# Attention and mixture-of-experts block on one core: the last batch's attention shares its slots with the first 38 dense units

## The chip, the cores and the metric

One core of a Trainium2 chip. The metric is the device time of one launch in microseconds (us). The engines are TensorE (PE; its weight loads are shown as PEld), VectorE (DVE), ScalarE (ACT), GpSimd (POOL) and SyncE (SP), which here only issues DMAs. Each engine takes its instructions strictly in program order; a semaphore wait holds everything behind it on its engine.

## What is computed

Four batches of 256 tokens with 256 channels (`x`, and a side input `f` of the same shape). Shortened:

```
# bi-directional WKV: two linear scans over the tokens, forward and backward
ek = exp(min(f, 30)); ekv = ek * f
nf, df = forward scans of ekv, ek;  nb, db = backward scans
num = nf + nb - ekv + exp(min(u + f, 30)) * f;  den = df + db - ek + exp(min(u + f, 30))
wkv(x) = sigmoid(x) * num / max(den, 1e-8) * (0.8 + 0.2 * tf)

qkv = wkv1(x) @ Wqkv.T + bqkv                     # 16 heads of 16 channels
x = x + softmax(q k.T * 4) v @ Wproj.T + bproj
h = wkv2(x)                                       # same scans with other w, u
scores = sigmoid(h @ gate_w.T)                    # 64 experts, 8 groups
w = best 6 experts out of the 4 best groups, normalised, times 2.5
x = x + sum_e w_e * relu(h @ w1_e.T)**2 @ w2_e.T + relu(h @ up.T)**2 @ down.T
```

All experts are computed for all tokens, each weighted by `w` (zero where it is not chosen).

## The kernel before

**Layout and stages.** Channels lie on the partitions, in two chunks (KC = 2), tokens in the free dimension. Batch b's scans feed two "hidden" tensors: `hid1` (attention input) and `hid2` (dense input). Each engine has its own hand-written instruction list; the order in these lists is the schedule.

**Attention.** `project` (L1129) makes q, k and v of a batch, 8 matmul instructions each. ACT rounds q and k to `qk_hi` (`evacuate_qk`, L495); DVE takes the low parts `qk_lo` (`split_qk`, L772) and adds the bias of v (`add_v_bias`, L785). SP stacks high and low parts in `q_st`/`k_st` (three slots of 8 heads). Per head there is `scores` (L1140, two matmuls), `maximum` on DVE (L796), `shifted_scores` (L1159, the scores again with the negative maximum added by two extra rows), `probabilities` on ACT (L511), and once per four heads `values` (L1172, 16 instructions). `scores` of head n waits for `maximum` of head n-2, since two PSUM banks take turns. After a batch: `turn_out`, `normalise`, `turn_normalised`, `evacuate_o_ch`, `project_out`, `residual`, `second_exp`, `second_rec`, `hidden2`, `gate`, `gate_exp`, `router` (32 DVE steps for one batch, 256 tokens), `turn_weights`, `evacuate_w`. This is called the tail of a batch here. Batch b's tail, and the second half of its heads, run while batch b+1's first half is made; the second scans of batch b+1 and the first scans of b+2 are spread between the maxima.

**Dense part.** 34 tiles of 128 intermediate channels (2 shared, 32 with two experts each), each applied to two halves of 512 tokens: 68 units. Unit n: SP loads the raw weights and the spread gates (`load_unit`); ACT rounds the weights (`split_hi`, L567) and DVE takes the rest (`split_lo`, L949); PE `up` (L1258 to L1260, 6 matmuls of 512 columns); ACT `rectify` (L574); POOL `square` (L446); DVE `gated` (L1053, times gates); ACT `round_act` (L581); DVE `low_act` (L1058); PE `down` (L1269 to L1271, 6 matmuls), two units later. The order of one unit's turn is, on every engine:

```
PE   up(n), down(n-2)
ACT  rectify(n), round_act(n-1), split_hi(n+2)
POOL square(n)
DVE  low_act(n-1), gated(n), split_lo(n+2)
```

The dense part begins when all attention scores of batch 3 are done; the first 18 units (HEAD) also hold the tail of batch 3, with three router steps behind each unit. Then loops of four units run to the end. `result` adds the sums to x1, and SP stores the output.

Of the kernel before, what the change touches and what calls it, by code (L numbers as in the profile page):

```python
# [17 lines left out]
P = 128  # L18
B, S, C = 4, 256, 256
# [12 lines left out]
HEAD = 18  # L32
# [7 lines left out]
RING = 4  # L40
PRING = 8
# [15 lines left out]
def bass_adaln_attn_ffn(nc, xT, fT, cond, vecs, w_in, w_out, gate_w, bv, gate_bias, tiles, out):  # L57
# [3 lines left out]
    with ExitStack() as ctx:  # L61
# [12 lines left out]
        cond_sb = sb("cond_sb", [P, B, TD])  # L74
# [22 lines left out]
        ekv = sb("ekv", [P, KC, S])  # L97
# [10 lines left out]
        ones = sb("ones", [2 * SHARED * B, S])  # L108
        zeros = sb("zeros", [MAXROW - STACK, S])
# [9 lines left out]
        o_ch = sb("o_ch", [P, KC, S])  # L119
# [3 lines left out]
        hid2 = sb("hid2", [P, KC, S])  # L123
        hid_hi = sb("hid_hi", [P, KC, TOK], F32R)
        hid_lo = sb("hid_lo", [P, KC, TOK], F32R)
        gex = sb("gex", [P, QT, E])
        gden = sb("gden", [P, QT, E])
        score = sb("score", [P, QT, E])
        sbias = sb("sbias", [P, QT, G, EG])
        pmax = sb("pmax", [P, QT * G, 4])  # L130
        pmin = sb("pmin", [P, QT * G, 4])
        qmax = sb("qmax", [P, QT * G, 2])
        qmid = sb("qmid", [P, QT * G, 2])
        qlow = sb("qlow", [P, QT * G, 2])
        qsec = sb("qsec", [P, QT * G, 2])
        fmax = sb("fmax", [P, QT * G, 1])
        fmid = sb("fmid", [P, QT * G, 1])
        flow = sb("flow", [P, QT * G, 1])
        fsec = sb("fsec", [P, QT * G, 1])
        gsum = sb("gsum", [P, QT, G + 4])  # L140
        gtop = sb("gtop", [P, QT, 8])
        grep = sb("grep", [P, QT, G + 4])
        gpen = sb("gpen", [P, QT, G])
        masked = sb("masked", [P, QT, E + 2])
        etop = sb("etop", [P, QT, 8])
        erep = sb("erep", [P, QT, E + 2])
        wsel = sb("wsel", [P, QT, E])
        wsum = sb("wsum", [P, QT])
        wsum1 = sb("wsum1", [P, QT])
        wrec = sb("wrec", [P, QT])  # L150
        wful = sb("wful", [P, QT, E])
        w_ch = sb("w_ch", [E, TOK])
# [3 lines left out]
        t_hi = k_st[:, 2].rearrange("p (k n) s -> p k (n s)", k=RING)  # L156
        t_lo = q_st[:, 2].rearrange("p (k n) s -> p k (n s)", k=RING)
# [8 lines left out]
        ones_ready, ld_ones = sem("ones_ready"), sem("ld_ones")  # L166
# [37 lines left out]
        def bank_s(n):  # L204
            return ps[:, n % 2, :].rearrange("p (t k) -> p t k", t=QT)
# [43 lines left out]
        def bank_h(k):  # L249
            return ps[:, k, :]  # L250
# [1151 lines left out]
```

## Time and profile before

| | us |
|---|---|
| median of 3 runs | 408.05 (405.69 to 408.51) |
| the profiled execution | 405.65 |
| its span, first to last instruction | 403.8 |
| PE / DVE busy in it | 317.7 (79%) / 322.9 (80%) |
| ACT / POOL busy | 201.2 (50%) / 129.5 (32%) |
| mean granted clock of TensorE | 0.897 of full speed |

The profile gives busy time by engine, the busy share in 40 slices of the span, the chain of work that ended last, and the costliest groups of instructions. Durations of neighbouring instructions on one engine overlap by some 0.07 us, so the distance from start to start is the cost of one, and that is what is used below. The granted clock is 1.0 where TensorE ran at 2.4 GHz and 0.5 where it ran at 1.2 GHz.

### The profile page before, as it was taken

Reading aid. Unit: us, or ns where it says so; the run is one execution under the profiler, and the core shown is the slowest. Engines: PE = TensorE matmul, PEld = TensorE weight load, DVE = VectorE, ACT = ScalarE, POOL = GpSimd, SP = SyncE. Lnnn points to the kernel's source line nnn. Section 1 sums busy time; section 2 is a strip of 40 time slices with the busy share of each in tenths; the row PEclk is TensorE's granted clock in tenths of the full one; section 3 lists DMA queues with packets and bytes.
Section 4 is the critical chain, followed back from the end, with each engine's and each line's share of the span. In section 5 each row is a group of like instructions: output and inputs, shape, how many; then the busy total and the mean of one; then the engine's idle time right before and its main releaser. Section 6 shows DMA issues by size and latency. Waiting matters only on the chain.

```text
span 403.8 us, 6023 instructions
## 1 busy us (share of the span) xinstructions
PE 317.7 (79%) x1552; PEld 244.3 (61%) x1552; DVE 322.9 (80%) x623; ACT 201.2 (50%) x373; POOL 129.5 (32%) x117
## 2 busy tenths in 40 slices
PE   0071369677954897768988897999999999999994
PEld 0050247455733585545666675888888788888882
DVE  6979997986699477886568995888888888888883
ACT  4112125434552256466455553666666666656651
POOL 3428443306061002011322342434334334334331
PEclk9995559758985798997999998999999999999999
DMA  6959707803380068300543444566556666656531
GB/s 199 164 71 119 166 2 93 111 11 52 55 106 2 13 94 105 108 10 24 173 144 117 157 168 145 163 188 192 194 181 194 177 200 188 199 182 191 195 139 52
DMA packets 36150, 50.89 MB, mean 126 GB/s; under 512 B 5218, under 2 KB 17954, under 8 KB 36130
## 3 DMA queue, kind: packets, MB, share of 16 engines
q1 hardware_dynamic: 36130, 50.65, 51.4%
q8 instruction: 9, 0.15, 0.2%
q14 instruction: 11, 0.09, 0.1%
HBM read 39.16 MB, written 1.33 MB: 100 GB/s over the span
## 4 chain that ended last, share of the span: by engine, by line
PE 54%; DVE 29%; issue 7%; ACT 5%; POOL 2%; DMA 1%; DVEq 0%; ACTq 0%; SPq 0%; POOLq 0%
DVE scan L731 7%; PE ps L1258 7%; PE ps L1260 7%; PE ps L1269 6%; PE ps L1271 6%; PE ps L1259 6%; PE ps L1270 6%; DVE mx L796 5%; PE ps L1129 4%; PE ps L1172 3%; PE ps L1140 2%; DVE q_st L949 2%; DVE scan L1053 2%; PE ps L1159 2%; DVE den L744 2%
## 5 line engine op out<-in xcount | busy, mean ns | idle before, releaser
L446 POOL TENSOR_TENSOR scan<-scan 128x512 f32<-128x512 f32 x68 | 73.2, 1076 | 137.9 <-ACT scan L574 136.2
L1058 DVE TENSOR_TENSOR qk_lo<-scan,qk_hi 128x512 fp32r<-128x512 f32 x68 | 69.3, 1019 | 31.3 <-ACT qk_hi L581 31.3
L574 ACT ACTIVATE scan<-ps 128x512 f32<-128x512 f32 x68 | 40.7, 598 | 49.8 <-PE ps L1260 49.6
L1140 PE MATMUL ps<-k_st,q_st 96*128 96x256 f32 x128 | 35.6, 395 | 30.8 <-DVE mx L796 20.3
L1269 PE MATMUL ps<-qk_hi,k_st 128*128 128x512 f32 x136 | 54.7, 402 | 4.5 <-DVE qk_lo L1058 4.3
L1258 PE MATMUL ps<-hid_hi,k_st 128*128 128x512 f32 x136 | 54.4, 400 | 2.0 <-DVE q_st L949 2.0
L567 ACT ACTIVATE k_st<-clip 128x512 fp32r<-128x512 f32 x68 | 42.8, 631 | 25.3 <-PE ps L1271 25.3
L1260 PE MATMUL ps<-hid_hi,q_st 128*128 128x512 f32 x136 | 54.0, 397 | 0.0
L1271 PE MATMUL ps<-qk_hi,q_st 128*128 128x512 f32 x136 | 53.7, 395 | 0.0
L1270 PE MATMUL ps<-qk_lo,k_st 128*128 128x512 f32 x136 | 53.6, 394 | 0.0
L1259 PE MATMUL ps<-hid_lo,k_st 128*128 128x512 f32 x136 | 53.6, 394 | 0.0
L511 ACT ACTIVATE prob<-ps 128x512 f32<-128x512 f32 x64 | 36.6, 593 | 33.5 <-PE ps L1159 33.0
L949 DVE TENSOR_TENSOR q_st<-clip,k_st 128x512 fp32r<-128x512 f32 x68 | 48.6, 716 | 2.6 <-ACT k_st L567 2.6
L1140 PEld LDWEIGHTS ps<-k_st,q_st 96*128 96x128 f32 x128 | 25.0, 255 | 40.9 <-DVE mx L796 27.9
L796 DVE TENSOR_REDUCE mx<-ps 128x2 f32<-128x512 f32 x64 | 42.6, 679 | 5.6 <-PE ps L1140 4.3
L1053 DVE TENSOR_TENSOR scan<-scan,ex 128x512 f32<-128x512 f32 x68 | 46.1, 679 | 0.2 <-DVE o_tok L816 0.2
L581 ACT ACTIVATE qk_hi<-scan 128x512 fp32r<-128x512 f32 x68 | 42.5, 624 | 2.8 <-DVE scan L1053 2.6
L1159 PE MATMUL ps<-q_st,k_st 98*128 98x256 f32 x128 | 33.5, 359 | 5.5 <-ACT prob L511 3.2
L1129 PE MATMUL ps<-hid,wi 128*128 128x256 f32 x64 | 20.3, 478 | 19.8 <-DVE hid L764 19.8
L1269 PEld LDWEIGHTS ps<-qk_hi,k_st 128*128 128x128 f32 x136 | 25.7, 189 | 14.5 <-DVE qk_lo L1058 8.2
L1258 PEld LDWEIGHTS ps<-hid_hi,k_st 128*128 128x128 f32 x136 | 25.8, 190 | 9.2 <-DVE q_st L949 3.5
L1159 PEld LDWEIGHTS ps<-q_st,k_st 98*128 98x128 f32 x128 | 24.6, 233 | 11.0 <-ACT prob L511 6.2
(117 smaller groups left out, 451.4 us busy)
## 6 DMA issues: line engine op xcount, KB each, us to landing
clip<-in_tiles SPq DMA_DIRECT2D x68, 256.0 KB, 3.1
ex<-gates SPq DMA_DIRECT2D x136, 128.0 KB, 2.9
q_st<-qk_hi SPq DMA_DIRECT2D x16, 128.0 KB, 3.9
q_st<-qk_lo SPq DMA_DIRECT2D x16, 128.0 KB, 4.5
k_st<-qk_hi SPq DMA_DIRECT2D x16, 128.0 KB, 5.3
k_st<-qk_lo SPq DMA_DIRECT2D x16, 128.0 KB, 6.2
f_sb<-in_fT SPq DMA_DIRECT2D x4, 256.0 KB, 8.8
x_sb<-in_xT SPq DMA_DIRECT2D x4, 256.0 KB, 9.6
```

The costliest lines, as they stand in the source:

```text
L446: g.tensor_tensor(sq[:, k], relu[:, k], relu[:, k], ALU.mult).then_inc(sq_ready, 1)
L796: v.tensor_reduce(mx[:, b % 2, h], bank_s(n), AX_X, ALU.max).then_inc(max_ready, 1)
L949: TT(t_lo[:, k], raw[:, k], t_hi[:, k].bitcast(F32), ALU.subtract).then_inc(t_lo_ready, 1)
L1058: TT(act_lo[:, k], act[:, k], act_hi[:, k].bitcast(F32), ALU.subtract).then_inc(act_lo_ready, 1)
L1140: last = mm(bank_s(n)[:, qt], q_st[0:MAXROW, slot(b, h // HB), h % HB, qt * P:(qt + 1) * P], k_st[0:MAXROW, slot(b, h // HB), h % HB, :], ...
L1159: last = mm(bank_t(n)[:, kt], k_st[0:MAXROW + 2, slot(b, h // HB), h % HB, kt * P:(kt + 1) * P], q_st[0:MAXROW + 2, slot(b, h // HB), h % ...
L1258: mm(bank_h(k), w_hi, x_hi, start=(c == 0), stop=False)
L1259: mm(bank_h(k), w_hi, x_lo, start=False, stop=False)
L1260: last = mm(bank_h(k), w_lo, x_hi, start=False, stop=(c == KC - 1))
L1269: mm(acc, w_hi, act_hi[:, k], start=first, stop=False, skip_group_check=True)
L1270: mm(acc, w_hi, act_lo[:, k], start=False, stop=False, skip_group_check=True)
L1271: last = mm(acc, w_lo, act_hi[:, k], start=False, stop=final, skip_group_check=True)
```

## The change

- The dense part's first 38 units no longer wait for batch 3's attention. Batches 0 to 2 run in 48 "slots", one head's `scores` and `maximum` in each. The 43 slots after that hold batch 3's 16 heads (slots 0 to 15) and units 0 to 37: unit n stands in slot n+4 (n < 2) or n+5. `shifted_scores`, `probabilities` and `values` lag `scores` by 10 slots.
- In those slots `scores` has a single PSUM bank (bank 0), so head n waits for the maximum of head n-1; `shifted_scores` has a single bank (2) from head 40 on; units 0 to 11 have a single bank (1) for `up`.
- The low parts of q and k of batches 1 to 3: PE subtracts the rounded part in PSUM (`subtract_high`: two matmuls with a negative identity), ACT evacuates (`evacuate_rest`). v's bias is added by a matmul, v evacuated by ACT.
- One router of the same steps for two batches (four token tiles): the first, `router(0)`, in slots 0 to 3 (6 steps each), the second in slots 33 to 36.
- The gates of a unit are loaded with one DMA, not two. Buffers are shared otherwise; the dense weights `t_hi`/`t_lo` have buffers of their own. `exponentials` is split and takes `clip[:, 3]` second; `ekv` lies in `clip[:, 3]`.
- The loops of four now cover units 38 to 65.

```diff
-HEAD = 18
+RT = 2 * QT
+LAG = 10
+ENTRY = 4
+GAP = 1
+ALONE = 12
+HEAD = NT + RING
...
         def bank_s(n):
-            return ps[:, n % 2, :].rearrange("p (t k) -> p t k", t=QT)
+            return ps[:, n % 2 if n < H * (B - 1) else 0, :].rearrange("p (t k) -> p t k", t=QT)
 
         def bank_t(n):
-            return ps[:, 2 + n % 2, :].rearrange("p (t q) -> p t q", t=QT)
+            return ps[:, 2 + n % 2 if n < H * (B - 1) - HB else 2, :].rearrange("p (t q) -> p t q", t=QT)
...
+        def unit_bank(n):
+            return n % 2 if n >= ALONE else 1
+
+        def unit_at(s):
+            n = s - ENTRY if s < ENTRY + SHARED else s - ENTRY - GAP
+            return n if n >= 0 and (s < ENTRY + SHARED or n >= SHARED) else None
+
+        def head_slot(n):
+            early = H + HB <= n < 2 * H
+            return H + HB + LAG + (n - H - HB) // 2 if early else n + LAG
+
+        def tail_slot(b):
+            return head_slot(H * b + H - 1) + 2
...
# SyncE
+            for n in range(RING, 2 * RING):
+                next_raw(n, n, n % RING)
             store_gates(0)
-            store_gates(1)
-            sp.wait_ge(st_gates, 32)
-            for n in range(RING):
+            for n in range(SHARED, RING):
                 load_spread(0, n, n)
...
# ScalarE
+            def evacuate_rest(b, w):
+
+                job = ("qk"[w], b)
+                sc.wait_ge(rest_ready, 2 * (b - 1) + w + 1)
+                for t in range(KC):
+                    u = (V_BQ, V_BK)[w] + t
+                    a.activation(qk_lo[:, w, t], job_bank(job)[:, t * S:(t + 1) * S], ACT.Identity,
+                                 bias=vec[:, u:u + 1]).then_inc(qk_lo_ready, 1)
...
+            for s in range(HEAD + ENTRY + GAP):
+                n = unit_at(s)
+                for m in shifted_at(H * (B - 1) + s):
+                    probabilities(m // H, m % H, m % H + 1)
+                if s < 2:
+                    split_hi(s, s, 1)
...
+                if n is not None:
+                    rectify(n, n % 2)
+                    if n > 0:
+                        round_act(n - 1, (n - 1) % 2)
+                    split_hi(n + 2, (n + 2) % RING, (n + 2) // RING + 1)
...
# VectorE
+            for g in range(H * (B - 1)):
+                b, s = g // H, g % H
+                maximum(b, s)
+                if s == 0:
+                    if b > 0:
+                        low_max(b - 1, 1)
+                    num_den(b + 1, 0, 0)
+                if s == 1:
+                    hidden1(b + 1)
+                if s == 2:
+                    scans(b + 1, 1, 1, 0)
...
+            route_now = router(0)
+            for s in range(HEAD + ENTRY + GAP):
+                n = unit_at(s)
+                if s < H:
+                    maximum(3, s)
+                if s == 0:
+                    low_max(2, 1)
+                if s < 2:
+                    split_lo(s, s)
+                if s < 4:
+                    for _ in range(6):
+                        next(route_now, None)
...
+                if n is not None:
+                    if n > 0:
+                        low_act(n - 1, (n - 1) % 2)
+                    gated(n, n % 2, n % RING, n // RING + 1)
+                    split_lo(n + 2, (n + 2) % RING)
...
# TensorE
+            def subtract_high(b, w):
+
+                job = ("qk"[w], b)
+                pe.wait_ge(qk_hi_ready, 4 * b + 2 * w + 2)
+                for t in range(KC):
+                    last = mm(job_bank(job)[:, t * S:(t + 1) * S], minus[:], qk_hi[:, w, t], start=False, stop=True,
+                              skip_group_check=True)
+                last.then_inc(rest_ready, 1)
...
-                    pe.wait_ge(max_ready, n - 1)
+                    pe.wait_ge(max_ready, n if n > H * (B - 1) else n - 1)
...
+            for g in range(H * (B - 1)):
+                b, s = g // H, g % H
+                for n in shifted_at(g):
+                    shifted_scores(n // H, n % H)
+                if g + 2 <= H * (B - 1):
+                    scores((g + 2) // H, (g + 2) % H)
+                for m in values_at(g):
+                    values(m // 4, m % 4)
+                if s == 2:
+                    project(b + 1, "q")
+                if s == 3:
+                    subtract_high(b + 1, 0)
+                if s == 4:
+                    project(b + 1, "k")
+                if s == 5:
+                    subtract_high(b + 1, 1)
...
+            for s in range(HEAD + ENTRY + GAP):
+                n = unit_at(s)
+                for m in shifted_at(H * (B - 1) + s):
+                    shifted_scores(m // H, m % H)
+                if s + 1 < H:
+                    scores(B - 1, s + 1)
+                if s == 4:
+                    turn_weights(0)
+                for m in values_at(H * (B - 1) + s):
+                    values(m // 4, m % 4)
...
+                up(n, n // NT, n % 2, n % RING)
+                if n >= 2:
+                    down(n - 2, (n - 2) // NT, n % 2, (n - 2) % RING, first=(n - 2) % NT == 0, final=n - 2 == NT - 1)
```

## Rows read from the trace of the kernel before

**Rows 1.** The page: PE's busy tenths in 40 equal slices, and granted TensorE clock

```profile
PE   0071369677954897768988897999999999999994
PEclk9995559758985798997999998999999999999999
```

**Rows 2.** Windows: busy us of PE, PEld, DVE, ACT, POOL; granted clock; DMA share

```profile
175.00:180.00 5.00, 3.08 (x28) 1.76 (x26) 3.93 (x13) 4.22 (x9) 0.33 (x1) 1.00 0.03 7
180.00:185.00 5.00, 3.52 (x20) 2.88 (x24) 2.42 (x6) 3.34 (x8) 2.20 (x2) 0.58 0.05 13
```

**Rows 3.** Timeline: first maxima of batches 0, 1, 3; first `up` matmul of units 0, 38, 67

```profile
42.48 0.68 DVE L796 TENSOR_REDUCE mx<-ps 128x2 f32<-128x512 f32 x1
...
74.77 0.68 DVE L796 TENSOR_REDUCE mx<-ps 128x2 f32<-128x512 f32 x1
...
155.27 0.68 DVE L796 TENSOR_REDUCE mx<-ps 128x2 f32<-128x512 f32 x1
...
192.89 0.50 PE L1258 MATMUL ps<-hid_hi,k_st 128*128 128x512 f32 x1
...
311.87 0.40 PE L1258 MATMUL ps<-hid_hi,k_st 128*128 128x512 f32 x1
...
392.19 0.40 PE L1258 MATMUL ps<-hid_hi,k_st 128*128 128x512 f32 x1
```

**Rows 4.** Timeline, DVE: two scans, a maximum, a stall at `split_qk`, a later maximum

```profile
43.08 1.26 DVE L731 TENSOR_TENSOR_SCAN scan<-ps,ex 128x256 f32<-128x256 f32 x2
44.26 0.66 DVE L796 TENSOR_REDUCE mx<-ps 128x2 f32<-128x512 f32 x1
...
62.70 0.88 DVE L772 SCALAR_TENSOR_TENSOR qk_lo<-ps,vec,qk_hi 128x256 fp32r<-128x256 f32 x2 [2.27 <-ACT qk_hi L495]
...
162.19 0.68 DVE L796 TENSOR_REDUCE mx<-ps 128x2 f32<-128x512 f32 x1
```

**Rows 5.** Timeline, PE: a `project`, `scores`, `shifted_scores`, `values`, the start of a tail

```profile
62.26 1.89 PE L1129 MATMUL ps<-hid,wi 128*128 128x256 f32 x8
...
162.93 0.50 PE L1140 MATMUL ps<-k_st,q_st 96*128 96x256 f32 x2 [0.17 <-DVE mx L796]
163.27 0.40 PE L1159 MATMUL ps<-q_st,k_st 98*128 98x256 f32 x2
...
165.58 1.07 PE L1172 MATMUL ps<-prob,v_aug 128*32 128x256 f32 x16
...
168.95 1.09 PE L1182 MATMUL ps<-ident,o_raw 128*128 128x128 f32 x8 [0.50 <-ACT o_raw L518]
```

**Rows 6.** Timeline, DVE: first and last step of a router of one batch

```profile
184.88 0.23 DVE L859 TENSOR_SCALAR gden<-gex 128x128 f32<-128x128 f32 x1 [2.49 <-ACT gex L549]
...
191.87 0.42 DVE L938 TENSOR_SCALAR wful<-wsel,wrec 128x64 f32<-128x64 f32 x2
```

**Rows 7.** Timeline of a dense unit in the steady part, all engines

```profile
300.79 0.40 PE L1258 MATMUL ps<-hid_hi,k_st 128*128 128x512 f32 x1
302.46 0.60 ACT L574 ACTIVATE scan<-ps 128x512 f32<-128x512 f32 x1 [0.78 <-PE ps L1260]
302.95 0.62 ACT L581 ACTIVATE qk_hi<-scan 128x512 fp32r<-128x512 f32 x1
303.13 1.04 POOL L446 TENSOR_TENSOR scan<-scan 128x512 f32<-128x512 f32 x1 [1.81 <-ACT scan L574]
303.61 1.11 DVE L1058 TENSOR_TENSOR qk_lo<-scan,qk_hi 128x512 fp32r<-128x512 f32 x1 [0.53 <-ACT qk_hi L581]
304.65 0.68 DVE L1053 TENSOR_TENSOR scan<-scan,ex 128x512 f32<-128x512 f32 x1
305.25 0.68 DVE L949 TENSOR_TENSOR q_st<-clip,k_st 128x512 fp32r<-128x512 f32 x1
```

**Rows 8.** Timeline, PE: two neighbouring matmuls of a unit at the low clock

```profile
246.24 0.63 PE L1269 MATMUL ps<-qk_hi,k_st 128*128 128x512 f32 x1
246.67 0.63 PE L1270 MATMUL ps<-qk_lo,k_st 128*128 128x512 f32 x1
```

More of the change, by code:

```diff
@@ new lines, in _ @@
+            for s in range(HB - 1, HEAD + 1):
+                if s + 1 >= 2 * RING and s + 1 < HEAD:
+                    n = s + 1
+                    next_raw(n, n % NT, n % RING)
+                n = s - 1
+                if n == NT + SHARED:
+                    store_gates(1)
+                if n >= RING + SHARED:
+                    next_spread(n, n // NT, n % NT, n % RING)
+                if s == HB - 1:
+                    load_rows(B - 1, 0)
+                if s == H - 1:
+                    load_rows(B - 1, 1)
@@ L571, in rectify @@
                 sc.wait_ge(h_ready, n + 1)
+                if isinstance(n, int) and n == 0:
+                    sc.wait_ge(numden_ready, 4 * B)
                 if not isinstance(n, int) or n >= 2:
                     sc.wait_ge(sq_ready, n - 1)
-                a.activation(relu[:, k], bank_h(k), ACT.Relu).then_inc(relu_ready, 1)
+                bank = unit_bank(n) if isinstance(n, int) else k
+                a.activation(relu[:, k], bank_h(bank), ACT.Relu).then_inc(relu_ready, 1)
             def round_act(n, k):
                 sc.wait_ge(act_ready, n + 1)
+                if isinstance(n, int) and n == 0:
+                    for half in range(KC):
+                        sc.wait_ge(ld_stack[slot(B - 1, half)], 128 * turn(B - 1, half))
                 if not isinstance(n, int) or n >= 2:
@@ L629, in _ @@
[L629 to L658 removed]
+                if s == 5:
+                    evacuate_rest(b + 1, 1)
@@ L1099, in loop @@
                         split_lo(n + 2, (first + k + 2) % RING)
[L1101 to L1107 removed]
+            loop(HEAD, UNITS - 2 - HEAD)
             for n in range(UNITS - 2, UNITS):
@@ L1315, in _ @@
-            for h in range(HB + 2, H):
-                shifted_scores(B - 1, h)
-            values(B - 1, 2)
-            values(B - 1, 3)
-            pe.wait_ge(hid_lo_ready, 2)
-            pe.wait_ge(hid_hi_ready, 2)
-            pe.wait_ge(max_ready, H * B)
-            up(0, 0, 0, 0)
-            turn_out(B - 1)
-            up(1, 0, 1, 1)
-            turn_normalised(B - 1)
-            for n in range(2, HEAD):
-                up(n, 0, n % 2, n % RING)
-                if n == 2:
-                    project_out(B - 1)
-                    turn_weights(B - 2)
-                if n == 6:
-                    gate(B - 1)
-                if n == 14:
-                    turn_weights(B - 1)
-                down(n - 2, 0, n % 2, (n - 2) % RING, first=(n == 2))
@@ L1355, in _ @@
+            for n in range(UNITS - 2, UNITS):
+                up(n, 1, n % 2, n % RING)
+                down(n - 2, 1, n % 2, (n - 2) % RING)
             for n in range(UNITS - 2, UNITS):
```

783 lines of the change are left out of this document (375 added, 408 removed).

## The prediction

> **What bounds the kernel now.** I read the page's slices first, then the timeline of each engine, and last the steady part of the dense stage. The page shows two regimes [rows 1]: up to about the nineteenth slice PE is busy in part and its clock drops to half again and again; after that it is nearly always busy at the full clock. The time marks [rows 3] cut the span in pieces. The first maximum of batch 0 starts at 42.5 us. Batch 0 lasts 32.3 us and batches 1 and 2 together 80.5, which makes 112.8 for three. Batch 3 takes 37.6 until unit 0 of the dense part starts at 192.9. Units 0 to 37 take 119.0, up to 311.9. From there 29 units to unit 67 take 80.3, so 2.77 us each, all of it PE's twelve matmuls, and 11.6 us remain after its start (span 403.8). The profiled run is 405.65, 1.85 more than its span and 0.6% under the median of 408.05. My sum is made against 405.65.
>
> So dense units cost 2.77 each when PE alone limits them, and the idle of PE lies in the 192.9 us before. The change tries to fill that idle by putting units beside batch 3's attention. What must be asked is how long one common slot is.
>
> **Three batches, 48 slots.** DVE loses the low parts of q and k: a pair costs 0.88 [rows 4], about 1.0 with its semaphore step, two pairs a batch. It loses the v bias, which I estimate as a little less than such a pair, 0.8. Together 2.8 a batch, 8.4 in three. The router of batch 0 that stood among batch 2's maxima goes too, 7.0 of the 7.4 us that a router takes alone (184.88 to 192.29 [rows 6]). 112.8 - 8.4 - 7.0 = 97.4. The wait of 2.27 us ahead of the low parts [rows 4] does not vanish: PE now waits for ACT's rounding before `subtract_high`, and the next `scores` stand behind it on PE, so DVE waits for those a little later. Its new PE work (two matmuls each for q and k) is a `scores` pair, 0.34 [rows 5] to 0.6 at the low clock; I add 0.6 net and take 98. The evacuations move to ACT, which is busy for half the span; they cost nothing while that holds, else some 2.5 a batch. The lag of 10 slots cannot remove a tail's chain: in batch 2 the maxima have little DVE work between them, and tail(1) has to pass through `hidden2` before router(0). From 168.95, the start of a tail [rows 5], to 184.88, the first router step [rows 6], the trace has 15.9 us. Bounds: 88, if every stall of three batches but some 12 us goes, and 113, if nothing is gained. The start up to 42.5 I leave as it is: a v bias less, one exponential more ahead of GpSimd.
>
> **Slots 0 to 3: router(0).** Four maxima at 0.6 (2.4), one `low_max` 0.4, two `split_lo` at 0.6 (1.2), the router, and 1.0 of waiting for the gate. The router has four tiles. If no step grew it would be 7.4, if all doubled 14.8. About half of its steps are one per tile and double; the others have a large fixed part. I take 11.7. Sum 16.7, of which PE sees almost nothing, so PE idles here.
>
> **Slots 4 to 15: the step on which it turns.** Here each slot has a maximum, a `scores` and a unit. I follow one slot from the start of maximum(s), with full-clock rows. `scores(s+1)` has one bank, so it waits for maximum(s): 162.19 to 162.93, 0.74 [rows 4, 5]. The next PE group starts 0.34 later [rows 5]. That is `up(n)`, which stands behind `scores` on PE; from its start to `rectify` 1.67 (300.79 to 302.46), to `round_act` 0.49, to `low_act` 0.66, `low_act` 1.04 (it runs beside POOL's `square`), `gated` 0.60, `split_lo` 0.60 [rows 7]. Only then does DVE reach maximum(s+1). The sum is 6.14 us, and none of it overlaps the next slot, because the ring is closed: maximum, `scores`, `up`, `rectify`, `round_act`, `low_act`, `gated`, `split_lo`, maximum. Before, the dense part had no such ring: nothing on PE waited for a DVE instruction that stood behind the same unit's `gated`. PE's own work in the slot is 2.77 plus two head pairs at 0.34 and a quarter of a `values` at 1.0 [rows 5], 3.7 us. So 2.4 us a slot are lost to the order.
>
> Slots 4, 5 and 7 to 14 are such, 10 x 6.1 = 61. Slot 6 has no unit: 1.6. Slot 15 has no `scores` behind it, so PE leaves it after about 3.9. On the ring between `scores` and `up` also lie `values` in slots 10 and 14 (2.0), tail(2)'s `turn_out` (1.0 [rows 5]), `turn_normalised` (0.5), `project_out` (1.75, as many instructions as the 1.89 of a `project` [rows 5]), and `turn_weights` (0.3): 5.6. That is 72. At the low clock matmuls are 0.43 apart (246.24 to 246.67 [rows 8]), against 0.23 at the full one; the six of `up` then cost 1.2 more and `scores` 0.25. The stage starts behind a long PE idle, so I give three slots of it, 4 us. Sum 76. Bounds: 65, if `low_act` is never slowed by POOL (0.4 less a slot) and the tail is hidden; 92, if the low clock rules throughout.
>
> **Slots 16 to 27.** The ring is open. PE: 12 units 33.2, ten `shifted_scores` at 0.34, three `values` 3.0, a gate 1.0, a `turn_out` 1.0: 41.6.
>
> **Slots 28 to 42.** 15 units 41.6, rest of tail(3) and `turn_weights` 3.5. Router(1), again 11.7, lies in four slots in which DVE has 0.53 to spare each (2.77 less 1.04 + 0.60 + 0.60 [rows 7]): 9 more. The chain over residual, two logarithms and `hidden2`: 2. Sum 56; bounds 50 and 61.
>
> **Sum.** 42.5 + 98 + 16.7 + 76 + 41.6 + 56 = 330.8 for the start of unit 38, which before was at 311.9. The rest is unchanged, 91.9 (80.3 + 11.6): span 422.7, time 424.6. I say 424. In short: the dense part starts some 35 us earlier and its first 38 units take some 53 us longer.
>
> **Edits at nothing.** One DMA in place of two for the gates: SP's time is not on the path in the steady part; where PE sets 2.77 a unit, the DMA's wait is covered. Buffers that share memory add waits only where the old user is long done. One I keep in mind: SP has `store_gates(0)` behind the raw loads of units 6 and 7, which wait for `split_lo` of units 2 and 3, that is for slots 4 and 5. The gates of unit 2 are then stored and read back while slot 6 and the first part of slot 7 pass, 6.5 us. It should just fit; if not, 2 to 4 us are lost once.
>
> **The rivals.**
>
> *The overlap works* (other side, faster). If the slots 4 to 15 ran at PE's own 3.7, 11 of them would save 26 us and the 4 us of low clock as well: 394. For it speaks that PE, ACT, DVE and POOL each have room; against it the order in the lists, which the rows price with hardly a free term. It decides below a mean slot of 4.4 us: the 18.9 us that I forecast as loss, over 11 slots, are 1.7 of 6.1. Chance 0.17.
>
> *The gains are larger and the loss smaller than I sum, to about no change*: three batches at the lower bound 88, router 8 instead of 11.7 twice. 424 - 10 - 7 = 407. Chance 0.13.
>
> *The low clock rules the common slots.* In the trace PE was busy 3.08 of 5 us at the full clock and idle for 2 us around 180; the next 5 us had a granted clock of 0.58, between the two levels of 2.4 and 1.2 GHz [rows 2]. A ring slot has a gap of 2.5 us on PE (from the end of `down` and `shifted_scores` at about 4.3 to 6.1 + 0.74). At 1.45 more for each of 11 slots, less the 4 counted, and as much again for the tail's instructions and slots 0 to 3: 424 + 12 + 4 = 440. Against it: at the low clock the PE work of a slot nearly fills it, and clock slices after such stretches come back to 9 [rows 1]. Chance 0.13.
>
> The Trainium skill, page "TensorE: Matmul & The Clock Gate", section "HAM oscillation — how this bites in real kernels", says that bursts of matmuls separated by waits can be throttled anew before each burst, so that every burst begins slow. By that rule this rival would come true in every ring slot; the window row agrees that one such gap was followed by a lower clock, though only once.
>
> *The first 48 slots gain nothing.* `project` (1.89, twice that at the low clock) and the wait before `subtract_high` stand ahead of `scores` in slots 2 to 5 and DVE waits as long as it did. 113 instead of 98: 439. Chance 0.09.
>
> My forecast: 0.48, with a range of its own of 412 to 436.
>
> **How the numbers follow.** A measurement of this kernel can tell about 1% from no change, so 404 to 412 is the same. Faster: the overlap (0.17) and a third of the second rival, 0.21. Same: the rest of it and the low end of mine, 0.14. Slower: 0.65. The range of 8 in 10 goes from 400, which leaves out most of the overlap case, to 440, which takes in the upper cases.
>
> **What would show it.** In the profile after: maxima of batch 3 from slot 4 on 6 us apart, with DVE idle ahead of `low_act` and released by `round_act`, and PE idle ahead of `scores`, released by the maximum; first maximum of batch 3 near 140; unit 0's `up` near 158; `up` of unit 38 near 331; from there 2.77 a unit. Maxima 4 us apart there would prove the ring wrong; a first maximum of batch 3 near 130 or 155 would put the error into the first 48 slots; unit periods of 2.77 through slots 33 to 36 would make the router's price wrong.

## The result and the profile after

| | before | after |
|---|---|---|
| median, us | 406.88 (405.69 to 408.51, 4 runs) | 627.77 (625.2 to 628.61, 4 runs) |
| ratio, 95% interval | | 1.541 (1.533 to 1.550) |
| span of the profiled execution, us | 403.8 | 626.1 |
| PE / DVE busy, us | 317.7 / 322.9 | 400.3 / 310.4 |
| mean granted clock | 0.897 | 0.793 |

The forecast was 424, the range 400 to 440. The direction was right; 204 us were missing from the sum.

The page of the changed kernel, the rows that answer to [rows 1], and the chain that ended last, by engine and by line:

```profile
PE   0526877688725646768985866672756566576664
PEclk9957567969657777778998976778878878778889
DMA 30%; SPq 28%; PE 18%; DVE 11%; issue 7%; ACT 3%; POOL 1%; DVEq 0%; ACTq 0%; POOLq 0%
SPq L305 20%; DMA ex<-gates 17%; SPq L309 5%; DMA q_st<-nmax_lo 5%; DMA clip<-in_tiles 4%; DMA k_st<-qk_lo 3%; PE ps L1188 3%; PE ps L1243 3%; SPq L343 2%; DVE mx L867 2%; DVE scan L814 2%; DVE t_lo L1019 2%; DVE scan L1098 2%; SPq L351 2%; PE ps L1211 2%
```

PE is no longer at 9 from the twentieth slice on, but at 5 to 7 up to the end. It is the second half, which the change hardly touches, that has got long. The chain names the queue of SP (28%) and the DMAs (30%), and in it two entries above all: L305, which issues the raw weights of a unit, and the gates' DMA.

Dense units in the loops, timeline of the changed kernel: one unit and the start of the next, the lines with waits and SP's issues (columns: start, duration, engine, line, operation, idle before and what ended it):

```profile
482.29 0.55 SPq L309 DMA_DIRECT2D ex<-gates  x1
483.11 4.80 SPq L305 DMA_DIRECT2D clip<-in_tiles  x1
485.72 0.63 ACT L637 ACTIVATE t_hi<-clip 128x512 fp32r<-128x512 f32 x1 [4.37 <-DMA clip<-in_tiles]
486.38 0.69 DVE L1019 TENSOR_TENSOR t_lo<-clip,t_hi 128x512 fp32r<-128x512 f32 x1 [3.26 <-ACT t_hi L637]
487.21 0.79 PE L1321 MATMUL ps<-hid_hi,t_hi 128*128 128x512 f32 x1 [2.97 <-DVE t_lo L1019]
488.11 0.55 SPq L309 DMA_DIRECT2D ex<-gates  x1
488.93 3.44 SPq L305 DMA_DIRECT2D clip<-in_tiles  x1
491.75 0.63 ACT L637 ACTIVATE t_hi<-clip 128x512 fp32r<-128x512 f32 x1 [4.39 <-DMA clip<-in_tiles]
```

A unit takes 491.75 - 485.72 = 6.0 us instead of 2.77. SP issues gates, then raw weights; the issue of the raw weights itself takes 4.8 and 3.4 us. ACT stands 4.4 us before the raw weights, DVE behind ACT, PE behind DVE. Before, ACT's rounding of the weights waited for PE only. The page's rows for it, first before, then after:

```profile
L567 ACT ACTIVATE k_st<-clip 128x512 fp32r<-128x512 f32 x68 | 42.8, 631 | 25.3 <-PE ps L1271 25.3
L637 ACT ACTIVATE t_hi<-clip 128x512 fp32r<-128x512 f32 x68 | 42.6, 627 | 155.3 <-DMA clip<-in_tiles 140.4
```

The pages' rows on DMAs: first before, then after (KB each, median us from issue to landing); the page after gives no landing for the gates:

```profile
clip<-in_tiles SPq DMA_DIRECT2D x68, 256.0 KB, 3.1
ex<-gates SPq DMA_DIRECT2D x136, 128.0 KB, 2.9
```

```profile
clip<-in_tiles SPq DMA_DIRECT2D x68, 256.0 KB, 14.6
ex<-gates SPq DMA_DIRECT2D x68, 256.0 KB
```

The raw weights' DMA has not been edited, and it lands 14.6 us after its issue instead of 3.1. What was edited is the DMA ahead of it in the queue. Bytes are the same (50.89 and 50.91 MB). 20 us of the loops, windows of before and of after (the last four columns: granted clock, DMA share, GB/s):

```profile
320.00:340.00 20.00, 20.00 (x88) 16.25 (x88) 16.61 (x22) 12.56 (x23) 7.93 (x8) 1.00 0.65 190
```

```profile
480.00:500.00 20.00, 11.42 (x39) 8.13 (x40) 8.52 (x11) 6.25 (x12) 4.20 (x4) 0.91 0.26 83
```

The 16 DMA engines are busy 26% of the time on average, not 65%, while everything waits for them: the mean of 16 would be as low as this if a few of them carried most of it. How many take part, the number of small packets suggests. Pages of the changed kernel, and of two variants of it that are described below: with two gate DMAs, and with one DMA of another shape:

```profile
DMA packets 33952, 50.91 MB, mean 81 GB/s; under 512 B 3146, under 2 KB 15626, under 8 KB 33930
```

```profile
DMA packets 35992, 50.92 MB, mean 110 GB/s; under 512 B 5186, under 2 KB 17666, under 8 KB 35970
```

```profile
DMA packets 34904, 50.91 MB, mean 111 GB/s; under 512 B 4098, under 2 KB 16578, under 8 KB 34882
```

Over 68 units the packets under 512 B are 5186 - 3146 = 2040 fewer than with two DMAs, 30 a unit; with the other shape they are 5186 - 4098 = 1088 fewer, 16 a unit. If every DMA engine that takes part in a DMA has one such packet, two DMAs have 32, one over all engines 16, and the one of the change 2. No view here names the engines, so the two engines are worked out from these counts. The new access pattern has a first dimension of 2, then 64 repeats, then 512 numbers. The Trainium skill, page "DMA: Bandwidth & Descriptors", section "Rules for kernel authors", says the same: a DMA whose outermost dimension is a small c, its example being a broadcast, runs on at most c of the engines. The trace agrees, with 2 small packets a DMA by this count and 6.0 us a unit.

### The profile page after: what moved, and what is told of

Same layout as the page of the kernel before. It is cut to its first block, busy times and chain, and to the rows that moved or that the text cites. A ratio compares the mean times of both kernels' runs of the same rounds, so it can differ in the third digit from the quotient of the medians.

```text
span 626.1 us, 5613 instructions
## 1 busy us (share of the span) xinstructions
PE 400.3 (64%) x1580; PEld 287.2 (46%) x1580; DVE 310.4 (50%) x552; ACT 203.9 (33%) x392; POOL 129.6 (21%) x117
## 2 busy tenths in 40 slices
DMA packets 33952, 50.91 MB, mean 81 GB/s; under 512 B 3146, under 2 KB 15626, under 8 KB 33930
## 4 chain that ended last, share of the span: by engine, by line
DMA 30%; SPq 28%; PE 18%; DVE 11%; issue 7%; ACT 3%; POOL 1%; DVEq 0%; ACTq 0%; POOLq 0%
SPq L305 20%; DMA ex<-gates 17%; SPq L309 5%; DMA q_st<-nmax_lo 5%; DMA clip<-in_tiles 4%; DMA k_st<-qk_lo 3%; PE ps L1188 3%; PE ps L1243 3%; SPq L343 2%; DVE mx L867 2%; DVE scan L814 2%; DVE t_lo L1019 2%; DVE scan L1098 2%; SPq L351 2%; PE ps L1211 2%
## 5 line engine op out<-in xcount | busy, mean ns | idle before, releaser
L1321 PE MATMUL ps<-hid_hi,t_hi 128*128 128x512 f32 x136 | 71.0, 522 | 91.2 <-DVE t_lo L1019 91.2
L1019 DVE TENSOR_TENSOR t_lo<-clip,t_hi 128x512 fp32r<-128x512 f32 x68 | 47.5, 699 | 102.8 <-ACT t_hi L637 102.7
L637 ACT ACTIVATE t_hi<-clip 128x512 fp32r<-128x512 f32 x68 | 42.6, 627 | 155.3 <-DMA clip<-in_tiles 140.4
L1321 PEld LDWEIGHTS ps<-hid_hi,t_hi 128*128 128x128 f32 x136 | 31.0, 228 | 117.6 <-DVE t_lo L1019 59.1
L1332 PE MATMUL ps<-qk_hi,t_hi 128*128 128x512 f32 x136 | 64.3, 473 | 7.4 <-DVE qk_lo L1103 7.3
L1323 PE MATMUL ps<-hid_hi,t_lo 128*128 128x512 f32 x136 | 65.4, 481 | 0.0
L1322 PE MATMUL ps<-hid_lo,t_hi 128*128 128x512 f32 x136 | 64.7, 476 | 0.0
L1333 PE MATMUL ps<-qk_lo,t_hi 128*128 128x512 f32 x136 | 61.7, 453 | 0.0
L1334 PE MATMUL ps<-qk_hi,t_lo 128*128 128x512 f32 x136 | 60.3, 443 | 0.0
L1332 PEld LDWEIGHTS ps<-qk_hi,t_hi 128*128 128x128 f32 x136 | 31.6, 233 | 20.9 <-DVE qk_lo L1103 13.0
## 6 DMA issues: line engine op xcount, KB each, us to landing
clip<-in_tiles SPq DMA_DIRECT2D x68, 256.0 KB, 14.6
```

The costliest lines, as they stand in the source:

```text
L1321: mm(bank_h(bank), w_hi, x_hi, start=(c == 0), stop=False)
L1322: mm(bank_h(bank), w_hi, x_lo, start=False, stop=False)
L1323: last = mm(bank_h(bank), w_lo, x_hi, start=False, stop=(c == KC - 1))
L1332: mm(acc, w_hi, act_hi[:, k], start=first, stop=False, skip_group_check=True)
L1333: mm(acc, w_hi, act_lo[:, k], start=False, stop=False, skip_group_check=True)
L1334: last = mm(acc, w_lo, act_hi[:, k], start=False, stop=final, skip_group_check=True)
```

## The experiments

Each time stands beside the kernel before, measured along with it (405.9 to 407.7).

**One: which edit costs the 204 us.** The changed kernel, with the gates loaded by two DMAs again (`e1_two_dmas`); the kernel before, with the one DMA of the change alone (`e2_before_one_dma`); and the changed kernel with one DMA of the same size whose first dimension is the 64 repeats (`e3_one_dma_64_first`). For the last one the two experts' rows of the weights alternate on the partitions, laid out so by the host. The edits, shortened (the semaphore counts and the layout are left out, `cols` stands for the slice of 512 tokens):

```diff
 # changed kernel
-sp.dma_start(spread[:, k], gates[t, :, cols].unsqueeze(1).broadcast_to([2, P // 2, HT]))
 # e1
+for r in range(2):
+    sp.dma_start(spread[r * (P // 2):(r + 1) * (P // 2), k], gates[t, r, cols].unsqueeze(0).broadcast_to([P // 2, HT]))
 # e3
+sp.dma_start(spread[:, k], gates[t, :, cols].unsqueeze(0).broadcast_to([P // 2, 2, HT]))
```

> The changed kernel with one edit undone: a unit's gates are loaded with two DMAs of 128 KB (one per expert row, each repeated over 64 partitions) as before, not with one of 256 KB. Theory A (the single gate DMA is the cause: its access pattern begins with a dimension of 2, the two rows, so that it is carried by few of the 16 DMA engines and takes about 6 us): unit period in the loops back to 2.77 us, raw weight loads land in about 3 us again instead of 14.6, time near 450 us (my 424 plus the 25 us that the first 48 slots took longer in the changed kernel, where no gate load ran yet). Theory B (the order of the slots is the cause, the DMAs only wait for it): the time stays above 580 us, unit period in the loops near 6 us.

Measured 462.59 (460.94 to 465.04), ratio 1.136 (1.129 to 1.142), span 463.3. The raw weights land in 3.0 us again and a unit of the loops takes 2.80, as theory A says; the time is 13 us above its 450.

> The kernel before with only the gate load changed: one DMA of 256 KB per unit in place of two of 128 KB. Theory A: all 68 units run at the pace of that DMA, 6.0 us each, from unit 0 at 192.9 us: 193 + 68 x 6.0 + about 10 = 611 us. Theory B: no change, 406 us; a small gain on SyncE (one issue of 0.5 us less per unit) is hidden.

Measured 613.34 (612.89 to 613.78), ratio 1.507 (1.498 to 1.516), span 611.1. The units take 5.98 us each in the loops, the raw weights land after 14.7 us, and the packets under 512 B are 3178 instead of 5218: 30 a unit fewer here too.

> The changed kernel with still one gate DMA of 256 KB per unit, but its pattern begins with the 64 repeats and has the two rows second; to match, the 128 rows of each weight tile are laid out alternating between the two experts. Same bytes, same count of DMAs, same packets of 2 KB. Theory A: as good as two DMAs, within 1% of e1_two_dmas, near 450 us, unit period 2.77 us. Theory C (a single DMA of this size with a repeated dimension is slow whatever the order of its dimensions, or its issue on SyncE is): as slow as the changed kernel, about 627 us.

Measured 459.09 (458.32 to 460.82), ratio 1.129 (1.123 to 1.136), span 457.3.

The one DMA costs the kernel before 207 us by itself, and taking it back gives the changed kernel 165. It isn't the merging: in the third shape the same 256 KB land in 3.3 us and the raw weights in 2.9. To separate this from the rest of the change, the kernel before got the third shape too (`e11_before_64_first`):

> The kernel before with one gate DMA per unit whose first dimension is the 64 repeats, instead of two DMAs. The form with first dimension 2 took it from 406 to 613. If the size of the first dimension alone is the cause (theory K), this one is at the kernel before, 402 to 408. If merging two loads costs by itself (a later landing of the half that was earlier), above 410.

Measured 406.71 (404.61 to 413.73, 12 runs), ratio 0.999 (0.996 to 1.002). One DMA in place of two is worth nothing here, as the prediction said, if its shape is right; its issue time was hidden anyway. The first dimension of 2 is the whole cost. The 3.5 us between the first and the third kernel are no gain of the DMA's shape as far as the profiles show: the 6.0 us between their spans stand in the first 48 slots (128.6 against 122.5), whose code is the same, and the intervals of the two ratios overlap.

**Two: the ring in slots 4 to 15.** From `e1_two_dmas`, with `scores(s+1)` issued behind the unit's `up` and `down` in the slots that hold a unit:

```diff
-                if s + 1 < H:
+                if s + 1 < H and n is None:
                     scores(B - 1, s + 1)
...
                 up(n, n // NT, n % 2, n % RING)
...
+                if s + 1 < H:
+                    scores(B - 1, s + 1)
```

> e1_two_dmas plus one more edit: in the common slots with a unit, TensorE issues the next head's scores behind up(n) and down(n-2), not ahead of them. Theory R (the ring maximum, scores, up, rectify, round_act, low_act, gated, split_lo closes in slots 4 to 15 and makes a slot 6.1 us): the ring opens, a slot falls towards 3.7 us, 20 to 26 us less than e1_two_dmas, near 425 us. Rival (the ring does not bind, the slots go at another pace): within 1% of e1_two_dmas.

Measured 430.37 (429.51 to 433.67), ratio 1.060 (1.054 to 1.067), span 427.7: 32 us less, where 20 to 26 were expected. Of the 35.6 us between the two spans 28.4 lie in slots 4 to 15, 2.4 in the 27 units behind them, and 5.1 in the first 48 slots, which the edit doesn't touch. One slot with the ring, slot 9, timeline of `e1_two_dmas`:

```profile
219.97 0.68 DVE L869 TENSOR_REDUCE mx<-ps 128x2 f32<-128x512 f32 x1
220.71 0.51 PE L1213 MATMUL ps<-k_st,q_st 96*128 96x256 f32 x2 [1.87 <-DVE mx L869]
221.05 0.40 PE L1323 MATMUL ps<-hid_hi,t_hi 128*128 128x512 f32 x1
221.28 0.39 PE L1324 MATMUL ps<-hid_lo,t_hi 128*128 128x512 f32 x1
221.78 0.63 PE L1323 MATMUL ps<-hid_hi,t_hi 128*128 128x512 f32 x1
222.21 0.63 PE L1324 MATMUL ps<-hid_lo,t_hi 128*128 128x512 f32 x1
223.30 0.60 ACT L649 ACTIVATE scan<-ps 128x512 f32<-128x512 f32 x1 [3.49 <-PE ps L1325]
223.80 0.62 ACT L659 ACTIVATE qk_hi<-scan 128x512 fp32r<-128x512 f32 x1
224.46 1.17 DVE L1105 TENSOR_TENSOR qk_lo<-scan,qk_hi 128x512 fp32r<-128x512 f32 x1 [3.80 <-ACT qk_hi L659]
225.55 0.68 DVE L1100 TENSOR_TENSOR scan<-scan,ex 128x512 f32<-128x512 f32 x1
226.31 0.69 DVE L1021 TENSOR_TENSOR t_lo<-clip,t_hi 128x512 fp32r<-128x512 f32 x1
226.92 0.68 DVE L869 TENSOR_REDUCE mx<-ps 128x2 f32<-128x512 f32 x1
```

And one without it, slot 8 of `e4_scores_behind_unit`:

```profile
202.70 0.68 DVE L869 TENSOR_REDUCE mx<-ps 128x2 f32<-128x512 f32 x1
203.74 1.18 DVE L1105 TENSOR_TENSOR qk_lo<-scan,qk_hi 128x512 fp32r<-128x512 f32 x1 [0.17 <-ACT qk_hi L659]
203.79 0.40 PE L1213 MATMUL ps<-k_st,q_st 96*128 96x256 f32 x2
204.26 0.39 PE L1323 MATMUL ps<-hid_hi,t_hi 128*128 128x512 f32 x1
205.44 0.68 DVE L1021 TENSOR_TENSOR t_lo<-clip,t_hi 128x512 fp32r<-128x512 f32 x1
206.04 0.68 DVE L869 TENSOR_REDUCE mx<-ps 128x2 f32<-128x512 f32 x1
```

Such a slot falls from 6.95 to 3.34 us, PE runs without a gap (203.79 to 207.07 between two `scores`), and DVE waits 0.17 instead of 3.80. Not every slot gains as much: from the maximum of slot 4 to that of slot 15 the mean slot is 7.20 us in `e1` and 4.49 in `e4`. The order in the list made the difference, not the engines' room.

**Three: the first 48 slots.** They took 124.0, 128.6 and 123.5 us in the profiles of the changed kernel, `e1` and `e4`, in which their code is the same; I had forecast 98. Three kernels on top of `e4` take PE's added work out again: v's bias added by DVE (`e5_v_on_dve`), the low parts of q and k on DVE (`e6_qk_low_on_dve`), both (`e7_both_on_dve`). A fourth then moves the projections of q and k from slots 2 and 4 to 4 and 6 (`e8_both_later`). The main lines of the edits:

```diff
 # e6, e7, e8 (VectorE; e8: s == 5 and 7)
+                if s == 4:
+                    split_qk(b + 1, 0)
+                if s == 6:
+                    split_qk(b + 1, 1)
 # TensorE, and evacuate_rest on ScalarE likewise
-                if s == 3:
-                    subtract_high(b + 1, 0)
-                if s == 5:
-                    subtract_high(b + 1, 1)
 # e5, e7, e8 (VectorE)
+                if s == (11, 11, 7)[b]:
+                    add_v_bias(b + 1)
```

> e4_scores_behind_unit with v's bias added by VectorE again (which also evacuates v), without the two one-row matmuls per v and ScalarE's evacuation. Theory P (in the first 48 slots TensorE's extra work stands ahead of the next scores and costs more than VectorE gains): the bias matmuls take 1.2 us each at the low clock, two per batch, and the wait of 4.5 us for the scores behind the v of batch 1 shrinks: 3 to 6 us less than e4. Rival D (VectorE is what limits these slots, work taken off it is a gain): 0.8 us per batch more, 2 to 3 us slower than e4.

Measured 431.32 (430.6 to 433.61), ratio 1.061 (1.055 to 1.067).

> e4_scores_behind_unit with the low parts of q and k on VectorE again (two slots behind their project), without subtract_high on TensorE and evacuate_rest on ScalarE. Theory P: TensorE no longer waits for ScalarE's rounding (7.1 us of waits in front of the subtract in e1, the longest 3.5 us, with scores queued behind it): 5 to 8 us less than e4. Rival D: 2.0 us of VectorE time per batch come back: up to 6 us slower than e4.

Measured 436.85 (430.52 to 438.12); one of the four runs is 5 us under the others, so no more than "not faster" is read from it.

> Both edits of e5 and e6 together. Theory P: 8 to 13 us less than e4, near 419 us. Rival D: 6 to 9 us slower than e4, near 438 us.

Measured 433.83 (431.71 to 434.85), ratio 1.064 (1.058 to 1.070).

> e7 with project q and k in slots 4 and 6 instead of 2 and 4 (and v of batch 3 in slot 7 instead of 6, the gate of batch 0 in slot 6). ScalarE's rounding of q must wait until the stack of the batch before is copied; in e1 it waited 15.9 us for these copies in two places. Theory S (this wait is passed on): 2 to 6 us less than e7. Rival (it is hidden by the rest of the slot): within 1% of e7.

Measured 442.41 (441.28 to 442.9), ratio 1.086 (1.081 to 1.092).

The added PE work is not the cause: without it the kernel is not faster. Two slots later for the projections made it worse by 8.6 us, which neither of the two theories had. That does not clear their early place: in the kernel before, the q of a batch is projected behind `scores` of head 11 of the batch before (`project(b + 1, "q")` at L1279), and no run puts it back there. What the profile says of the stage stands in the waits of DVE. Before, 42.5 to 155.3 us (columns: waiting instruction, what ended the wait, us in total, times, longest):

```profile
DVE qk_lo L772 <- ACT qk_hi L495: 9.8, 5, 2.7
DVE mx L796 <- PE ps L1140: 3.4, 3, 2.0
```

and in `e4`, 42.3 to 165.8 us:

```profile
DVE mx L869 <- PE ps L1213: 20.3, 10, 4.5
DVE nmax_lo L874 <- ACT nmax_hi L572: 9.2, 4, 4.9
DVE x_sb L898 <- PE ps L1276: 5.5, 2, 3.7
DVE rsum L887 <- PE ps L1255: 5.1, 2, 4.8
```

The windows of the same two stretches (busy us of PE, PEld, DVE, ACT, POOL):

```profile
42.50:155.30 112.80, 80.28 (x446) 59.53 (x446) 91.14 (x198) 46.06 (x95) 33.17 (x26) 0.75 0.42 64
```

```profile
42.30:165.80 123.50, 90.99 (x461) 64.08 (x461) 78.02 (x142) 50.48 (x108) 32.87 (x26) 0.76 0.43 64
```

DVE's work fell by 13.1 us, close to the 15.4 that the prediction took off. Its idle time rose from 21.7 to 45.5 us, at a granted clock that is the same. So the question became what the waits stand for. Theory: the steps stand one slot behind their producers, too near. `e9_consumers_later` moves them one slot on:

```diff
-                if s == 8:
+                if s == (9, 9, 8)[b]:
                     low_max(b, 0)
-                if s == 3:
+                if s == 4:
                     subtract_high(b + 1, 0)
-                if s == 5:
+                if s == 6:
                     subtract_high(b + 1, 1)
...
-                    if t == 1:
+                    late = int(c == 0)
+                    if t == 1 + late:
                         normalise(c)
```

and likewise `low_max(b - 1, 1)`, the rest of batch 0's tail, and their steps on ScalarE. `e10_best_changed` is the same with the gates in one DMA of the third shape.

> The kernel with two gate DMAs and scores behind the unit (427.7 span, 430.4), with the steps that consume another engine's result moved one slot further from their producer in the first 48 slots: the low part of the first maxima in slot 9 instead of 8 (batches 0 and 1), of the second maxima in slot 1 instead of 0, subtract_high of q and k two slots after their projections instead of one, batch 0's normalise, transposition, residual and hidden2 one slot later each. Nothing is computed differently. In the trace of the kernel it starts from, DVE was busy 78.0 of the 123.5 us of the 48 slots and idle 45.5 us; before it was busy 91.1 of 112.8 and idle 21.7. Theory N (the steps stand too close to their producers in the in-order lists, so each wait stops all heads): the waits ahead of nmax_lo (9.2 us), rsum (5.1), and half of those of maxima for scores (20.3) mostly go, 12 us or more; batch 3's first maximum near 154 and the time near 418 or less. Theory L (the work of a slot in a chain PE, ACT, DMA sets the pace, with stacked slots of q and k coming free ten slots later, so that the stack's DMAs land late and ACT's qk_hi waits 8.3 us for them whatever the order): the waits reappear elsewhere, time 427 or more.

Measured 431.24 (430.28 to 433.53, 6 runs), ratio 1.061 (1.057 to 1.065).

> The kernel with the later consumers and, on top, the gates of a unit in one DMA whose first dimension is the 64 repeats (the weights' rows are laid out alternately for the two experts). The single DMA of that form took 3.5 us off the kernel with two DMAs (462.6 to 459.1). If that adds, 3 to 4 us under the kernel with later consumers. If gate loads are hidden once scores no longer hold up the units: no difference between the two.

Measured 431.92 (428.13 to 433.72, 6 runs), ratio 1.063 (1.057 to 1.068): no difference from `e9`.

The time of `e9` is that of `e4`, so by its number the theory falls. Its profile says why in part: batch 2 began at 115.6 instead of 122.8 us, and then 9 us were lost in one place:

```profile
134.27 0.84 ACT L540 ACTIVATE qk_hi<-ps,vec 128x256 fp32r<-128x256 f32 x2 [7.94 <-DMA k_st<-qk_lo]
135.27 0.64 ACT L609 ACTIVATE den<-den 128x512 f32<-128x512 f32 x1
135.94 0.75 DVE L918 SCALAR_TENSOR_TENSOR hid<-num,cfac,den 128x512 f32<-128x512 f32 x1 [8.88 <-ACT den L609]
```

ACT may not write the next `qk_hi` before the DMAs that stack the last one have landed. These stand on SP behind `load_rows`, which waits for the maxima of slot 15, and so are issued in slots 0 and 1; the projection of the next q now stands in slot 2. Before, it stood behind `scores` of head 11, late in a batch. ACT stopped 8.3 and 7.5 us there in `e4`, and everything behind it on ACT too. The chain of waits over the three batches, by line, is led in the kernel before by DVE's scans (17.1%) and maxima (14.9%), and the stacking DMAs don't stand among its first eleven; in `e4` `project` leads with 16.6%, then those DMAs' landing with 15.8% and their issue with 10.2%. Two kernels were to tell whether this stop is the price of the stage. `e12_tail_ahead` puts the end of tail(0) (`second_exp`, `second_rec`, `hidden2`) back ahead of it; `e13_qk_later` also moves the projections so that the DMAs have landed or nearly. One of the four lines of `e12`, and those of `e13`:

```diff
 # e12
-                    if t == 6 + late:
+                    if t == 6:
                         second_rec(c)
 # e13, both on TensorE and ScalarE
-                if s == 2:
+                if s == (4, 4, 3)[b]:
                     project(b + 1, "q")
-                if s == 4:
+                if s == (6, 6, 5)[b]:
                     subtract_high(b + 1, 0)
                     project(b + 1, "k")
-                if s == 6:
+                if s == (8, 8, 6)[b]:
                     subtract_high(b + 1, 1)
```

> The kernel with later consumers (431.2; batches begin at 42.3, 73.7, 115.6, 167.9), with second_exp, second_rec and hidden2 of batch 0 back one slot, so that ACT's second_rec(0) stands ahead of the evacuation of batch 3's q, before which ACT waits for the stack's DMAs (8.6 us in one). Theory W (ACT's list, stopped by that wait, is what holds DVE): the 8.9 us ahead of hidden2 go and nothing of this size takes their place; batch 3 begins near 159, time 421 to 424. Theory G (batch 2 is paced by something else, the wait only stands where slack was): 428 or more.

Measured 431.57 (430.61 to 432.72, 6 runs), ratio 1.062 (1.059 to 1.066).

> The same, with the projections of q and k in slots 4 and 6 (batches 0 and 1) and 3 and 5 (batch 2) instead of 2 and 4, and their evacuations and subtractions as much later; the low parts still by TensorE and ScalarE. The stack's DMAs, issued in slots 0 and 1, have then landed or nearly so when ACT comes to qk_hi. Theory W: ACT's waits for them (16.6 us in two) fall to 8 or less and the batches get shorter, 3 to 8 us under the kernel without this shift. Theory G, or a stack that now lands too late for the next batch's first scores (waits of PE at scores for the DMA): no gain or a loss.

Measured 428.59 (425.17 to 431.14, 6 runs), ratio 1.055 (1.049 to 1.060), span 423.4.

In `e12` the 8.9 us ahead of `hidden2` are gone, and DVE's waits ahead of maxima rose from 19.2 to 27.3: nothing gained, as theory G says. In `e13` ACT's waits for the stacking DMAs fell from 16.2 to 9.3 us (expected: to 8 or less), and the time by 3.0, at the low end of what I had expected if the stop were the price, with intervals that just overlap. The largest waits of ACT in its first three batches:

```profile
ACT qk_hi L540 <- PE ps L1191: 14.3, 4, 9.3
ACT v_aug L563 <- PE ps L1194: 13.4, 3, 6.3
```

So the stop may be a part of it, of about 3 us and not of 25. The rest stays open: the waits move between DVE, PE and ACT, and those that I took away were made up for at other instructions. No run shows one cause that owns it. Three parts of the change were never taken back in these slots: the lag of 10 slots between `scores` and `shifted_scores`, the place of the projections as it was, and the order of all other steps among the slots. They are the rivals that remain.

No version beats the kernel before. The best of the changed ones is `e13`, 5.5% slower.

## Why the prediction was right or wrong

The prediction's pieces against three profiles. The marks are DVE's first maxima of batches 0 and 3, its maximum of slot 4, and the `gated` of units 11, 38 and 67; the prediction's piece for slots 4 to 15 has 3.9 us added for the way from `up` to `gated` [rows 7].

| us | predicted | after | e1 | e4 |
|---|---|---|---|---|
| up to the first maximum | 42.5 | 41.3 | 41.4 | 42.3 |
| 48 slots | 98 | 124.0 | 128.6 | 123.5 |
| slots 0 to 3, router(0) | 16.7 | 23.0 | 17.9 | 17.5 |
| slots 4 to 15, to `gated` of unit 11 | 79.9 | 102.0 | 88.0 | 59.6 |
| 27 units to unit 38 | 97.6 | 156.0 | 98.4 | 96.0 |
| 29 units to unit 67 | 80.3 | 171.8 | 81.1 | 81.0 |
| rest | 7.7 | 7.9 | 7.9 | 7.8 |
| span | 422.7 | 626.1 | 463.3 | 427.7 |

The marks that carry the largest piece, in the changed kernel:

```profile
446.42 0.68 DVE L1098 TENSOR_TENSOR scan<-scan,ex 128x512 f32<-128x512 f32 x1
618.20 0.69 DVE L1098 TENSOR_TENSOR scan<-scan,ex 128x512 f32<-128x512 f32 x1
```

**The step that failed: "Edits at nothing. One DMA in place of two for the gates: SP's time is not on the path ... the DMA's wait is covered."** It priced the issue and took the transfer as unchanged because the bytes are. The diff's `broadcast_to([2, P // 2, HT])` put a dimension of 2 first, and 256 KB a unit then went through two DMA engines, by the count of small packets. 163 of the 204 us are this (626.1 - 463.3). The trace of before could have priced it: in its loops, shown above, the 16 engines move 190 GB/s at a share of 0.65, which makes 292 GB/s for all of them and 36 for two. 256 KB, 262 thousand bytes, then take 7.2 us against a unit of 2.77. That is an estimate made afterwards, and the 6.0 measured lie near it. No rival named this edit either, and each was worked out from the places that the change was about.

**Three batches in 98: wrong, and on the wrong side of its bounds (88 to 113).** The work taken from DVE was priced well (13.1 against 15.4). The step that failed is the subtraction itself: "112.8 - 8.4 - 7.0 = 97.4" holds if DVE sets the pace and its waits stay what they were. In the kernel before it was idle for 21.7 of 112.8 us. After the change it was idle for 45.5 of 123.5, of which 20.3 ahead of maxima for `scores`, against 3.4 before. Why these waits grew stays open. The first maximum of batch 3 came at 165.4 us in the changed kernel, past the 155 that the prediction named as a sign of an error here. The rival "the first 48 slots gain nothing" (0.09) had the right sign, and DVE does wait for `scores`; it stopped at 113, and they lost another 11. The cause that it names, projections and the wait before `subtract_high` ahead of `scores` on PE, is not shown: without the subtraction (`e6`) nothing was gained, two slots later for the projections cost 8.6 us in `e8`, and in `e13` the shift gained 3.0. PE's busy time rose by 10.7 us where I had a few matmuls at 0.6 net, and `e5` to `e7` show that taking that work out buys nothing.

**Slots 4 to 15 in 76, and 6.14 a slot: the mechanism right, shown by the second experiment, the size low.** The ring ran as described, link by link. The slot shown took 6.95: from `up` to `rectify` 2.25 instead of 1.67, and `split_lo` 0.76 behind `gated` instead of 0.60, since ACT's rounding of the weights came late. The first is the low clock, which set in within `up`: its first matmuls start 0.23 us apart, those from 221.78 on 0.43. I had counted the low clock for three slots. The granted clock in `e1` was 0.50 in slots 4 and 5, 0.75 to 0.83 in slots 7 to 10 and 14, and 1.00 in slots 11 to 13. One slot of each kind, windows of `e1` (slots 5, 9 and 12; the third column from the end is the granted clock):

```profile
195.80:203.31 7.51, 3.78 (x10) 2.91 (x10) 2.92 (x5) 2.12 (x4) 1.04 (x1) 0.50 0.09 35
219.97:226.92 6.95, 5.08 (x16) 3.96 (x16) 3.07 (x6) 2.23 (x4) 1.04 (x1) 0.75 0.21 75
242.82:249.40 6.58, 3.99 (x20) 3.24 (x20) 2.99 (x6) 2.83 (x5) 1.04 (x1) 1.00 0.29 82
```

Slot 12, at the full clock, has 6.58 instead of 6.14, and 0.36 of the difference stands between `scores` and `up`, where four matmuls of a tail lie. The rival "The low clock rules the common slots" (440, 0.13) describes this in part: the whole piece took 8.1 us more than forecast, about half of its price of 16, and not all of that is the clock. The Trainium skill's rule that stood beside it (page "TensorE: Matmul & The Clock Gate", section "HAM oscillation — how this bites in real kernels") would have each burst begin slow. The trace of this stage does not show that. In slots 8 to 14 the `scores` pair that opens the slot runs at the full pace, 0.50 or 0.51 us, behind waits of 1.87 to 2.60 us; the clock falls later in the slot (8 to 10 and 14) or not at all (11 to 13, each behind a wait of 2.59). From the maximum of slot 4 to that of slot 15 the granted clock was 0.79 in `e1` and, without these waits, 0.91 in `e4`.

**"The overlap works" (0.17)** is not what this kernel did. `e4`, which opens the ring, comes near it: the slot shown takes 3.3 us, the mean of the eleven 4.49, just above the 4.4 below which the rival decides. Its piece is 20.3 us under my forecast, where the rival put 30. That kernel is 6% slower than before all the same, since the 48 slots lose 11 us against before and the whole plan rests on their gaining 15.

**Slots 16 to 42 and the loops: right, slots 0 to 3 right by luck in part.** The 27 units took 98.4 and 96.0 against 97.6. Slots 0 to 3 took 17.9 and 17.5 against 16.7 where the gate DMA doesn't reach (23.0 in the changed kernel), but two misses offset each other: in `e1` the router's own steps take about 10 us instead of 11.7, and DVE waits 4.0 us in slot 0 instead of 1.0. In `e1` DVE waits nowhere for the gates' DMAs, so `store_gates(0)` fitted ahead of its unit, as the prediction had it.

With the gate DMA in either good form, the forecast of 424 would have stood against 463 and 459, both above its range: the sum was too low by 40.6 in `e1`, of which 30.6 lie in the 48 slots.

## What to carry to other kernels

Ask of every DMA in a diff which dimension comes first in its pattern, before asking how many bytes it moves or what hides its issue: a merged transfer with a first dimension of 2 held up an untouched transfer behind it from 3.1 to 14.6 us and the kernel by half. Work taken from an engine shortens a stage only as long as that engine sets its pace; ask what its next wait will be for, and price that. A consumer with a single buffer closes a ring through every engine that stands between in the lists, and moving its producer behind the independent work, here three lines, was worth some 30 us, 28.4 of them in its own stage.

## What the runs showed that I had not expected

- The queue of SP stopped at the issue of an instruction: with the narrow DMAs ahead of it the issue of the raw weights took 4.8 us where it takes 0.33 in `e1_two_dmas`. Over the changed kernel's loops its median is 4.8, and in `e2_before_one_dma` 4.9. So this DMA costs the issuing engine time too, at the next one.
- The small packets differ by 30 and 16 a unit between the three shapes, which fits 32, 16 and 2, one for each DMA engine that a transfer uses.
- The same 48 slots took 122.5, 123.5, 124.0 and 128.6 us in four profiled executions of kernels that don't differ there, so a difference under some 5 us in this stage isn't read from one profile.
